# Attention scores on a quarter of the contraction rows each, four head pairs side by side

## The reference

```python
Q = split_heads(query @ Wq + bq)
K = split_heads(key @ Wk + bk)
V = split_heads(value @ Wv + bv)
scores = jnp.einsum('bhqd,bhkd->bhqk', Q, K) / jnp.sqrt(jnp.float32(D))
attn = jax.nn.softmax(scores, axis=-1)
out = jnp.einsum('bhqk,bhkd->bhqd', attn, V)
out = out.transpose(0, 2, 1, 3).reshape(B, S, E)
return out @ Wo + bo
```

## Time and profile before

| | us |
|---|---|
| median of 3 runs | 2665.74 |
| lowest, highest | 2662.6, 2667.45 |
| profiled execution, span | 2662.7 |
| PE busy | 2428.4 (91%) |
| DVE busy | 1555.2 (58%) |
| ACT busy | 824.2 (31%) |
| POOL busy | 505.4 (19%) |
| HBM | 43 GB/s |

### The profile page before, as it was taken

How to read it: one execution, slowest core, us unless ns; L and a number is a source line. 1 busy time by engine, 2 the same in 40 slices (tenths; PEclk the granted TensorE clock), 3 DMA queues, 4 the chain that set the end, 5 groups by cost and what they waited for, 6 DMA issues and landing times. The chain is left out here.

```text
span 2662.7 us, 40410 instructions
## 1 busy us (share of the span) xinstructions
PE 2428.4 (91%) x15047; PEld 2099.3 (79%) x15047; DVE 1555.2 (58%) x3192; ACT 824.2 (31%) x1090; POOL 505.4 (19%) x414
## 2 busy tenths in 40 slices
PE   5999999663599985999999959999999999999999
PEld 3888888643588983888888748888888888888888
DVE  5777777479454535777667555444444444444444
ACT  1343434202354431333333333222222222222222
POOL 3222222005566642222222131000000000000000
PEclk8999999775799997999999969999999999999999
DMA  2111111210344331111111131000000000000000
GB/s 67 33 63 47 63 55 48 64 17 1 102 93 91 68 45 34 48 47 59 52 55 40 40 122 36 24 24 24 24 24 24 20 19 21 19 19 20 24 24 16
DMA packets 117469, 114.39 MB, mean 43 GB/s; under 512 B 15440, under 2 KB 114320, under 8 KB 117392
## 3 DMA queue, kind: packets, MB, share of 16 engines
q1 hardware_dynamic: 105104, 96.29, 11.4%
q0 software_dynamic: 12288, 17.05, 3.8%
HBM read 62.72 MB, written 50.59 MB: 43 GB/s over the span
## 5 line engine op out<-in xcount | busy, mean ns | idle before, releaser
L1751 DVE TENSOR_TENSOR zmix_hid<-zmix_act_gate,psum 128x1024 f32<-128x1024 f32 x128 | 156.3, 1221 | 406.2 <-issue 386.8
L140 PE MATMUL psum<-zmix_wd_hi,zmix_hid_hi 128*128 128x256 f32 x1024 | 289.5, 283 | 1.7 <-DVE zmix_acc L1742 1.7
L141 PE MATMUL psum<-zmix_wd_lo,zmix_hid_hi 128*128 128x256 f32 x1024 | 289.9, 283 | 0.0
L142 PE MATMUL psum<-zmix_wd_hi,zmix_hid_lo 128*128 128x256 f32 x1024 | 289.9, 283 | 0.0
L1698 ACT ACTIVATE zmix_act_gate<-psum 128x1024 f32<-128x1024 f32 x128 | 131.7, 1029 | 411.4 <-PE psum L142 411.4
L1706 ACT ACTIVATE zmix_hid_hi<-zmix_hid 128x1024 fp32r<-128x1024 f32 x128 | 135.5, 1059 | 388.0 <-PE psum L142 285.7
L582 PEld LDWEIGHTS psum<-att_v_cur,att_probs 128*128 128x128 f32 x2048 | 248.2, 192 | 6.6 <-ACT att_probs L683 0.2
L582 PE MATMUL psum<-att_v_cur,att_probs 128*128 128x96 f32 x2048 | 245.2, 273 | 0.0
L1756 DVE TENSOR_TENSOR zmix_hid_lo<-zmix_hid,zmix_hid_hi 128x1024 fp32r<-128x1024 f32 x128 | 158.1, 1235 | 134.8 <-ACT zmix_hid_hi L1706 133.9
L1742 DVE SCALAR_TENSOR_TENSOR zmix_acc<-psum,zmix_weight,zmix_acc 128x256 f32<-128x256 f32 x512 | 211.6, 475 | 1.6 <-PE psum L142 1.6
L140 PE MATMUL psum<-zmix_xT_hi,zmix_wg_hi 128*128 128x512 f32 x512 | 203.7, 398 | 8.4 <-DVE zmix_xT_lo L1730 4.6
(11 more groups left out here) (281 smaller groups left out, 5287.7 us busy)
## 6 DMA issues: line engine op xcount, KB each, us to landing
x<-att_x_new SPq DMA_DIRECT2D x32, 512.0 KB, 2.9
att_x_in<-in_x SPq DMA_DIRECT2D x16, 512.0 KB, 3.9
rows<-att_normed_new SPq DMA_DIRECT2D x16, 512.0 KB, 3.0
att_x_in<-x SPq DMA_DIRECT2D x16, 512.0 KB, 3.9
normed<-att_normed_new SPq DMA_DIRECT2D x16, 512.0 KB, 2.9
zmix_xn<-normed SPq DMA_DIRECT2D x16, 512.0 KB, 4.4
zmix_acc<-x SPq DMA_DIRECT2D x16, 512.0 KB, 4.0
out_x<-zmix_acc SPq DMA_DIRECT2D x16, 512.0 KB, 3.2
```

The lines of the kernel that those rows point to most:

```text
L140: pe.matmul(out, st_hi, mv_hi, start=first, stop=False)
L141: pe.matmul(out, st_hi, mv_lo, start=False, stop=False)
L142: return pe.matmul(out, st_lo, mv_hi, start=False, stop=last)
L1751: dve.tensor_tensor(hid[:, :, :], act_gate[:, :, :], psum[:, 2:4, :], ALU.mult).then_inc(up_out, 1)
```

## The change

`scores` takes a chunk of four head pairs at once. Pair j of the chunk has its 32 rows at partitions 32j to 32j + 31, and each of its matmuls reads those rows alone, of keys and of queries, and writes its own bank, 2 + j. The first pass is issued for all four pairs, then the second, the third and the subtraction of the maxima. In layer 1 four mask matmuls over 128 rows end the block. For the subtraction the maxima of a pair must lie in the pair's own 32 rows: `s_max` gets 4 groups of 32 columns, of which four columns each are used (two per chunk), all 128 are transposed and copied, and `negsel` is built anew. There are two blocks instead of three groups of pairs: the third, ahead of the maxima, is gone, and the exps on ACT are four and four. `maxima` waits for exps in banks 2 and 3, the second block for the first four exps.

```diff
--- before.py
+++ after.py
@@ -37,6 +37,8 @@
 PE_COLS = 96
 RSQRT_MAGIC = float(0x5F3759DF)
 NEWTON = 3
+ROWS = 2 * DH
+PAIR_ROWS = P // ROWS
 
 
 def done(count_per_batch, b, k):
@@ -148,7 +150,7 @@
 
     ident, headmask, negsel, keysel = const["ident"], const["headmask"], const["negsel"], const["keysel"]
     made, ident_made = sc.sem("const_made"), sc.sem("ident_made")
-    negf = sc.sb("negsel_f", [P, NP, P])
+    negf = sc.sb("negsel_f", [P, KC, P])
     keyf = sc.sb("keysel_f", [P, H // 2, SK])
 
     def identity(pool):
@@ -159,7 +161,7 @@
 
     def selectors(pool):
         pool.memset(headmask[:, :], 1.0).then_inc(made, 1)
-        pool.memset(negf[:, :, :], -1.0).then_inc(made, 1)
+        pool.memset(negf[:, :, :], 0.0).then_inc(made, 1)
         pool.memset(keyf[:, :, :], 0.0).then_inc(made, 1)
         pool.wait_ge(made, 3)
 
@@ -169,10 +171,11 @@
         pool.affine_select(out=keyf[:, :, :], in_=keyf[:, :, :], compare_op=ALU.not_equal, fill=1.0, base=0,
                            pattern=[[0, HH], [-1, SK]], channel_multiplier=1).then_inc(made, 1)
 
-        v = negf[:, :, :].rearrange("p j (a k) -> p j a k", a=2)
-        pool.affine_select(out=v, in_=v, compare_op=ALU.is_equal, fill=0.0, base=0,
-                           pattern=[[-2, NP], [-1, 2], [0, SK]], channel_multiplier=1).then_inc(made, 1)
-        pool.wait_ge(made, 6)
+        v = negf[:, :, :].rearrange("p c (a k) -> p (c a) k", a=2)
+        for j in range(PAIR_ROWS):
+            pool.affine_select(out=v, in_=v, compare_op=ALU.not_equal, fill=-1.0, base=-ROWS * j,
+                               pattern=[[-1, 2 * KC], [0, SK]], channel_multiplier=1).then_inc(made, 1)
+            pool.wait_ge(made, 6 + j)
         pool.affine_select(out=headmask[:, :], in_=headmask[:, :], compare_op=ALU.is_ge, fill=0.0, base=DH - 1,
                            pattern=[[DH, HH]], channel_multiplier=-1).then_inc(made, 1)
         pool.tensor_copy(negsel[:, :, :], negf[:, :, :]).then_inc(made, 1)
@@ -386,7 +389,7 @@
         qT_hi, qT_lo = sc.sb("qT_hi", [P, 2, KC, S], F32R), sc.sb("qT_lo", [P, 2, KC, S], F32R)
         kb_hi, kb_lo = sc.sb("kb_hi", [P, 2, KC, HH, SK], F32R), sc.sb("kb_lo", [P, 2, KC, HH, SK], F32R)
         v_cur = sc.sb("v_cur", [P, 2, (NP - 1) * 2 * VW + PE_COLS])
-        s_max = sc.sb("s_max", [P, TT, H])
+        s_max = sc.sb("s_max", [P, TT, PAIR_ROWS, ROWS])
         maxT = sc.sb("maxT", [P, S], F32R)
         probs = sc.sb("probs", [P, NP, S])
         recip = sc.sb("recip", [P, TT, H])
@@ -481,7 +484,7 @@
 
         @block.gpsimd
         def _(pool):
-            pool.memset(maxT[:, :].bitcast(F32), 0.0).then_inc(cleared, 1)
+            pool.memset(s_max[:, :, :, :], 0.0).then_inc(cleared, 1)
             pool.memset(v_cur[:, :, NP * 2 * VW:], 0.0).then_inc(cleared, 1)
             if masked:
                 pool.memset(mask_cur[:, :, :], 0.0).then_inc(cleared, 1)
@@ -533,6 +536,7 @@
                     pe.wait_ge(q_hi, done(KC, b, KC))
                     pe.wait_ge(kb_ready, done(2 * KC, b, 2 * KC))
                     after(pe, max_ready, b)
+                    after(pe, exp_done, done(NP, b - 1, PAIR_ROWS + 2))
                     if masked:
                         pe.wait_ge(mask_ready, b + 1)
                 for t in tiles:
@@ -548,23 +552,30 @@
             def turn_maxima(b):
                 pe.wait_ge(s_taken, done(TT * KC, b, TT * KC))
                 for t in range(TT):
-                    m = pe.transpose(psum[0:H, 3, t * P:(t + 1) * P], s_max[:, t, :], ident[:, :])
+                    m = pe.transpose(psum[:, 3, t * P:(t + 1) * P], s_max[:, t, :, :].rearrange("p j r -> p (j r)"), ident[:, :])
                 m.then_inc(max_turned, 1)
 
-            def scores(b, p, pairs):
-                if 0 in pairs:
+            def scores(b, p, c):
+                if c == 0:
                     pe.wait_ge(q_lo, done(KC, b, KC))
                     pe.wait_ge(max_ready, b + 1)
                     after(pe, lg_out, b - 1)
-                for j in pairs:
-                    after(pe, exp_done, done(NP, b, j - 1))
-                    c, heads = j // (NP // KC), slice(2 * (j % (NP // KC)), 2 * (j % (NP // KC)) + 2)
-                    out = psum[:, 4 + j % 2, :]
-                    three_passes(pe, out, kb_hi[:, p, c, heads, :], kb_lo[:, p, c, heads, :],
-                                 qT_hi[:, p, c, :], qT_lo[:, p, c, :], True, False)
-                    if masked:
-                        pe.matmul(out, const["keysel"][:, 0:2, :], mask_cur[:, p, :], start=False, stop=False)
-                    pe.matmul(out, const["negsel"][:, j, :], maxT[:, :], start=False, stop=True).then_inc(st_made, 1)
+                else:
+                    pe.wait_ge(exp_done, done(NP, b, c * PAIR_ROWS))
+                quarters = [(psum[:, 2 + j, :], slice(j * ROWS, (j + 1) * ROWS), slice(2 * j, 2 * j + 2)) for j in range(PAIR_ROWS)]
+                for out, rows, heads in quarters:
+                    pe.matmul(out, kb_hi[rows, p, c, heads, :], qT_hi[rows, p, c, :], start=True, stop=False)
+                for out, rows, heads in quarters:
+                    pe.matmul(out, kb_hi[rows, p, c, heads, :], qT_lo[rows, p, c, :], start=False, stop=False)
+                for out, rows, heads in quarters:
+                    pe.matmul(out, kb_lo[rows, p, c, heads, :], qT_hi[rows, p, c, :], start=False, stop=False)
+                for out, rows, heads in quarters:
+                    m = pe.matmul(out, const["negsel"][rows, c, :], maxT[rows, :], start=False, stop=not masked)
+                    if not masked:
+                        m.then_inc(st_made, 1)
+                if masked:
+                    for out, rows, heads in quarters:
+                        pe.matmul(out, const["keysel"][:, 0:2, :], mask_cur[:, p, :], start=False, stop=True).then_inc(st_made, 1)
 
             def weighted_values(b, p, t):
                 if t == 0:
@@ -618,15 +629,14 @@
 
             def body(b, p, half):
                 nxt = there(b + 1)
-                scores(b, p, range(0, 2))
+                scores(b, p, 0)
                 if there(b - 1):
                     outputs(b - 1)
                 if nxt:
                     turn_input(b + 1, 1 - p)
-                scores(b, p, range(2, 5))
+                scores(b, p, 1)
                 if nxt:
                     queries(b + 1, 1 - p)
-                scores(b, p, range(5, 8))
                 for t in range(TT):
                     if nxt:
                         maxima(b + 1, 1 - p, [t])
@@ -680,7 +690,7 @@
                     after(act, av_made, done(TT, b, 0))
                 for j in pairs:
                     act.wait_ge(st_made, done(NP, b, j + 1))
-                    act.activation(probs[:, j, :], psum[:, 4 + j % 2, :], ACT.Exp, scale=DH ** -0.5).then_inc(exp_done, 1)
+                    act.activation(probs[:, j, :], psum[:, 2 + j % PAIR_ROWS, :], ACT.Exp, scale=DH ** -0.5).then_inc(exp_done, 1)
 
             def new_copy(b):
                 act.wait_ge(new_turned, b + 1)
@@ -702,13 +712,12 @@
                     act.activation(aT_hi[:, c, :], psum[:, c, :], ACT.Copy).then_inc(a_hi, 1)
 
             def body(b, p, half):
-                exps(b, range(0, 2))
+                exps(b, range(0, 4))
                 if there(b + 1):
                     input_hi(b + 1, 1 - p)
-                exps(b, range(2, 5))
+                exps(b, range(4, 8))
                 if there(b + 1):
                     queries_hi(b + 1, 1 - p)
-                exps(b, range(5, 8))
                 if there(b - 1):
                     new_norm(b - 1, 1 - p, half + p - 1)
                     new_copy(b - 1)
@@ -775,13 +784,13 @@
                 for t in tiles:
                     for c in range(KC):
                         dve.wait_ge(s_made, done(TT * KC, b, t * KC + c + 1))
-                        s = psum[:, 2 + c, :].rearrange("p (h k) -> p h k", k=SK)
-                        dve.tensor_reduce(s_max[:, t, c * HH:(c + 1) * HH], s, AX.X, ALU.max).then_inc(s_taken, 1)
+                        s = psum[:, 2 + c, :].rearrange("p (j a k) -> p j a k", a=2, k=SK)
+                        dve.tensor_reduce(s_max[:, t, :, 2 * c:2 * c + 2], s, AX.X, ALU.max).then_inc(s_taken, 1)
 
             def maxima_copy(b):
                 dve.wait_ge(max_turned, b + 1)
                 after(dve, st_made, done(NP, b, 0))
-                dve.tensor_copy(maxT[0:H, :], psum[0:H, 3, :]).then_inc(max_ready, 1)
+                dve.tensor_copy(maxT[:, :], psum[:, 3, :]).then_inc(max_ready, 1)
 
             def normalise(b, t):
                 if t == 0:
@@ -1793,7 +1802,7 @@
     with ExitStack() as ctx:
         sc = Scope(nc, ctx, "main")
         const = {"ident": sc.sb("ident", [P, P]), "headmask": sc.sb("headmask", [P, HH]),
-                 "negsel": sc.sb("negsel", [P, NP, P], F32R), "keysel": sc.sb("keysel", [P, HH, SK], BF16)}
```

(1 more changed line is left out.)

## The result

The changed kernel takes 2598.72 us (2597.2 to 2599.27, four runs) beside 2664.76 us on the same chip: a ratio of 0.9753, interval 0.9739 to 0.9767. It is 66 us faster.

A forecast was written before the change was run, and what follows sets the result against it. PE was taken to set the pace, its score matmuls covering waits on DVE. 16 batches x (0.85 us in layer 0 + 1.9 in layer 1) = 44 us; 2662.7 - 44 + 3.0 = 2622 us, range 2604 to 2662.

The forecast's parts named there:

- part 1: Score matmuls on PE, both layers: 0.11 us each instead of 0.23, a block of 16 in 1.76 us instead of 3.68.
- full-overlap rival: Score matmuls on different rows run fully beside each other, 0.058 us each: 54 us gained, 2612 us; chance 0.21.
- part 2: Layer 0, where the blocks stand: waits on DVE and ACT remain, gain 0.85 us a batch.
- The three starts: Layer 0: projection waits for aT_lo, queries for nT_lo, maxima for q_hi, after about 0.9 us.
- the marker: Start of a batch's second weighted values on PE: from 222.99 to 222.15 in layer 0, 1211.79 to 1209.9 in layer 1.
- part 3: Layer 1: projection starts 0.3 us later, queries end at 1204.3, gain 1.9 us a batch.
- the DVE chain: Layer 1, DVE's work through the layer norm's end: shifts with the projection, 0.3 us later, L753 ending at 1207.95.
- part 4: ACT, both layers: four exps in a row, 2.4 us, ahead of qT_hi; cover only just enough, 0.2 us delay costs nothing.
- part 5: Score banks, copy and transposes of the maxima, constants: all at nothing, 0.1 us for the transposes at most.
- No overlap (rival): Score matmuls stay at 0.23 us each: 51 us slower, 2717 us; chance 0.15 together with a falling clock.
- Drain (rival): PE loses 0.16 us at each height change: 2628 us, or 2645 with matmuls at 0.15; with slower matmuls chance 0.13.
- The clock: Rival: the granted clock falls because PE gets gaps of up to 1 us; no price, chance 2 in 100.

The follow-up runs named there:

- experiment 1: The changed kernel with every score matmul at full height again (128 rows, negsel rebuilt), in the new order, banks and waits: 2699.34 us.
- Experiment 6: The changed kernel with layer 1's four full-height mask matmuls spread between the passes of each block instead of behind them: 2618.86 us.
- experiment 3: The changed kernel with 16 more 32-row matmuls ahead of the second block, all on rows 0 to 31 and into one bank: 2714.83 us.

## Why the prediction was wrong

- **The cost of a score matmul (part 1): mis-sized.** 0.11 us was taken from loads that follow one another on the whole array; measured 0.058. That is the full-overlap rival's figure. By the prediction's own sums this is 54 - 44 = 10 us, all of it in layer 1, and the rival's 0.21 was low: what spoke against it was a floor measured on another kind of load.
- **Layer 0 (part 2): right.** The three starts stayed with DVE and ACT: projection behind aT_lo, queries behind nT_lo, maxima 0.95 us behind the queries, L762 at 14.47 us. The gain was 0.90 us at the marker and 0.99 in the period, for 0.85. The cost of a matmul did not matter here, as the prediction says: by its own sums layer 0 gains 0.85 at 0.11 us and at 0.058.
- **Layer 1 (part 3): the step that failed.** "And with it the DVE chain" held the time from nT_lo to L753 fixed. Before, DVE stopped in the middle of it for qT_hi, with these rows of the timeline of the kernel before:

```profile
1199.82 1.22 DVE L764 TENSOR_TENSOR att_nT_lo<-psum,att_nT_hi 128x1024 fp32r<-128x1024 f32 x1 [1.32 <-ACT att_nT_hi L671]
...
1205.63 0.75 DVE L769 SCALAR_TENSOR_TENSOR att_qT_lo<-psum,att_bq_col,att_qT_hi 128x512 fp32r<-128x512 f32 x1 [0.56 <-ACT att_qT_hi L676]
```

From the start of nT_lo to the end of L753 are 7.83 us before (median over the batches of layer 1), 7.19 after; in layer 0 7.25 and 7.19. The queries were late there because PE was, so the wait was PE's time in disguise and went with the score matmuls: 0.64 us x 16 = 10 us. It comes back when the queries are pushed late again: 7.43 with the longer second block, 8.94 at full height (both layer 1). The full-overlap sum missed 16 x (3.16 - 2.5) = 11 us in layer 1 and 2 in layer 0; that is the 13 us between 2612 and 2599. Part 3 also calls aT_lo no bound for layer 1's projection; it is the bound now, as the rows above show. That cost little, since the full-overlap sum has the projection 2.08 us behind the block's start, and 2.13 were measured.
- **ACT (part 4) and the small edits (part 5): right.** Four exps in a row take 2.07 us and hold up nothing; the copy on 128 rows takes 0.69 us.
- **No overlap (rival): wrong of the quarters, right of the order.** Quarter-height matmuls do overlap. What the new order costs without that, it reckoned at 51 us over the kernel before; full height cost 34.
- **Drain (rival): real, and of the size that it took.** The eight transposes ahead of the second block take 0.96 us up to its start (205.62 to 206.58) where they took 0.79, so the change to quarter height costs 0.17 us; at full height in the same order (experiment 1) they take 0.79 again. Experiment 6 gives 0.155 a change, and the rival took 0.16. In layer 0 what the changes cost falls into waits.
- **The clock: did not fall** in the changed kernel (1.00 from 100 to 430 us and from 1041 to 1436 us); it did in experiment 3.

## What to carry to other kernels

When the engine that sets the pace gets cheaper, first list the waits that its work covered; they cap the gain, and reordering them can then be worth a good part of the change again: 43 us here beside 66. The exchange of transposes and projection, 34 us of these 43, was tried in the kernel before too and gave nothing there. A chain on another engine that stops for the engine being sped up isn't of fixed length: look inside it for such a stop before holding it fixed. Of a new form of instruction take both ends seriously, and don't price it by the floor of the old form.

## What was not expected of the hardware

- Matmuls on different 32-row quarters start out of program order: four pairs issued pair by pair run as fast as four side by side (2596.72 and 2598.72 us), and three quarters pass the last extra matmuls of the fourth. Rows and banks were never separated in these runs.
- Four loads of 128 columns and four matmuls of 512 on the four quarters cost 0.23 us together, what one costs on the whole array.
- Changing between full and quarter height costs about 0.16 us a change: 0.17 at the start of the second block, and 0.155 in experiment 6 (six changes in 0.93 us).
- Quarter-height matmuls one at a time for 3.7 us a batch were in some batches followed by a stretch at 1.2 GHz with PE as busy as in the others (clock 0.89 over 30 us, and 31.68 us for a batch instead of 28.48).
